# Layer 0 of a two-layer graph network: in the steps whose two MLP buffers have equal widths, one clamp and one logarithm instruction cover both

## The reference, cut to what matters

```python
def _L0_gnn_ref(x, edge_idx, W0, b0, W1, b1, W2, b2):
    row, col = (edge_idx[0], edge_idx[1])
    h = jnp.concatenate([x[row], x[col]], axis=-1)
    h = jax.nn.softplus(h @ W0 + b0)
    h = jax.nn.softplus(h @ W1 + b1)
    h = h @ W2 + b2
    return jax.ops.segment_sum(h, row, num_segments=x.shape[0])

h = jnp.maximum(_layernorm(x, axis=-1), 0.0)
x = x + _L0_gnn_ref(h, edge_index, L0_gnn_W0, ...)
```

## Time and profile before

| | us |
|---|---|
| median of 3 runs | 2696.3 |
| lowest, highest run | 2668.45, 2700.9 |
| the profiled execution | 2709.65 |
| its span, first to last instruction | 2708.0 |
| steady part of `edges0` (46 blocks) within that span | 379.3 to 1831.1 |

### The profile page before, as it was taken

The page is one execution under the profiler, slowest core; times in us unless marked ns, Lnnn a source line. Parts: engine busy times, 40 slices in busy tenths (PEclk is TensorE's granted clock), DMA queues, the critical chain, the costliest instruction groups (busy, mean ns, idle before and its releaser), DMA issues. The chain is left out here.

```text
span 2708.0 us, 37399 instructions
## 1 busy us (share of the span) xinstructions
PE 1645.4 (61%) x9524; PEld 1173.3 (43%) x9524; DVE 1475.0 (54%) x4143; ACT 977.4 (36%) x2307; POOL 1200.3 (44%) x1151
## 2 busy tenths in 40 slices
PE   0111277777777777777777777775354555645556
PEld 0111155555555655555555655554232323323334
DVE  6999556655555556555566555655233433333334
ACT  0566444444444444444444444442011111111134
POOL 0899633434333333433334433332655655655610
PEclk9999988888888878888898878887677777777775
DMA  1334213222222223222232222232222222222229
GB/s 38 111 121 125 78 43 75 60 56 58 57 56 56 64 67 61 59 58 57 64 72 58 59 56 56 56 69 56 41 51 44 50 48 44 50 45 47 50 79 307
DMA packets 345722, 183.07 MB, mean 68 GB/s; under 512 B 283916, under 2 KB 309913, under 8 KB 345671
## 3 DMA queue, kind: packets, MB, share of 16 engines
q1 hardware_dynamic: 292388, 119.46, 17.5%
q0 software_dynamic: 32928, 37.40, 8.5%
q10 hardware_dynamic: 20354, 25.65, 2.6%
HBM read 126.61 MB, written 55.79 MB: 67 GB/s over the span
## 5 line engine op out<-in xcount | busy, mean ns | idle before, releaser
L770 POOL DMA_INDIRECT fast_gathered<-h_table,fast_gather_i x588 | 569.5, 969 | 954.8 <-DVE fast_gather_i L784 787.2
L1120 POOL DMA_INDIRECT fast_gathered<-h_neighbours_table,fast_index_i x441 | 422.3, 958 | 344.8 <-issue 221.2
L791 DVE TENSOR_SCALAR fast_e<-fast_e 128x384 f32<-128x384 f32 (+1 forms) x490 | 194.9, 400 | 658.0 <-ACT fast_e L1028 582.3
L1028 ACT ACTIVATE fast_e<-bank,b_s 128x384 f32<-128x384 f32 (+1 forms) x490 | 295.2, 621 | 566.2 <-remote 306.3
L799 DVE SCALAR_TENSOR_TENSOR fast_h<-bank,b_s,fast_e 128x384 f32<-128x384 f32 (+1 forms) x490 | 303.5, 659 | 0.6 <-ACT fast_e L1035 0.6
L959 PE MATMUL bank<-fast_h,w_s 128*128 128x384 f32 (+1 forms) x490 | 275.0, 649 | 1.9 <-DVE fast_h L799 1.9
L1203 PE MATMUL bank<-fast_z_in,gw_s 128*128 128x512 f32 x98 | 92.4, 1043 | 289.3 <-ACT fast_z_in L1218 217.8
L1035 ACT ACTIVATE fast_e<-fast_e 128x384 f32<-128x384 f32 (+1 forms) x490 | 265.0, 560 | 6.9 <-issue 0.7
L945 PE MATMUL bank<-fast_in_t,w_s 128*128 128x384 f32 x294 | 163.8, 645 | 166.5 <-issue 86.4
L1218 ACT ACTIVATE fast_z_in<-node_sums 128x512 f32<-128x512 f32 x49 | 29.3, 597 | 635.2 <-DMA h_table<-prep_normed 589.8
L997 PE MATMUL node_sums<-fast_message,fast_hot 128*128 128x80 f32 x1568 | 227.5, 298 | 12.1 <-issue 12.1
(11 more groups left out here) (226 smaller groups left out, 3086.9 us busy)
## 6 DMA issues: line engine op xcount, KB each, us to landing
fast_local<-local_rows SPq DMA_DIRECT2D x49, 384.0 KB
h_neighbours_table<-fast_h_rows SPq DMA_DIRECT2D x49, 320.0 KB
fast_self_rows<-h_neighbours_table SPq DMA_DIRECT2D x49, 320.0 KB
h_table<-prep_normed ACTq DMA_DIRECT2D x49, 256.0 KB
fast_own_rows<-h_table SPq DMA_DIRECT2D x49, 256.0 KB
x_plus_h<-fast_x SPq DMA_DIRECT2D x49, 256.0 KB
finish_resid<-x_plus_h SPq DMA_DIRECT2D x49, 256.0 KB
prep_xin<-in_x SPq DMA_DIRECT2D x48, 256.0 KB
```

The lines of the kernel that those rows point to most:

```text
L770: pool.indirect_dma_start(gathered[slot][:, at:at + D], None, h0_t, bass.IndirectOffsetOnAxis(ap=gather_i[q][:, n:n + 1], axis=0))\
L791: V.tensor_scalar(e[at][:, 0:w], e[at][:, 0:w], EXP_CLAMP, None, ALU.min).then_inc(done, 1)
L1028: A(e[at][:, 0:w], psum[:, 0:w], ACT.Exp, bias=b_s[:, :]).then_inc(done, 1)
L1120: pool.indirect_dma_start(gathered[q][:, c * MW:(c + 1) * MW], None, h1_t, bass.IndirectOffsetOnAxis(ap=index_i[q][:, c:c + 1], axis=0))\
```

## The change

The two buffers of the exponentials become one buffer `e` of two halves of 512 columns (in each of two slots). In step i the first layer's exponential goes to the first half of the slot, the second layer's to the second half of the same slot. Where the two widths are equal (steps 1, 3 and 4: `is_joined`), one clamp and one logarithm instruction run over both halves. In steps 0 and 2 there are two of each as before. In a joined step both softplus instructions wait for the one logarithm (`l2_ready`), and the clamp waits for both exponentials.

```diff
-                in_t, e1, h1, e2, h2 = (t(n, [128, 512], 2) for n in ("in_t", "e1", "h1", "e2", "h2"))
+                in_t, h1, h2 = (t(n, [128, 512], 2) for n in ("in_t", "h1", "h2"))
+                e = t("e", [128, 2 * 512], 2)
...
+                def first_e(i, q):
+                    return e[slot_of(i, q)][:, 0:width(i)]
+
+                def second_e(p, q):
+                    return e[1 - slot_of(p, q)][:, 512:512 + width(p)]
+
+                def both_e(i, q):
+                    return e[slot_of(i, q)][:, :].rearrange("p (h w) -> p h w", h=2)[:, :, 0:width(i)]
+
+                def is_joined(i):
+                    return i > 0 and width(i) == width(i - 1)
...
+                        def clamp_both(i):
+                            def body(b, q, turn):
+                                dve.wait_ge(e1_ready, NU * b + i + 1)
+                                dve.wait_ge(e2_ready, NU * b + i)
+                                V.tensor_scalar(both_e(i, q), both_e(i, q), EXP_CLAMP, None, ALU.min).then_inc(m2_ready, 1)
+                            return body
+
+                        def softplus_first(i):
+                            def body(b, q, turn):
+                                if is_joined(i):
+                                    dve.wait_ge(l2_ready, NU * b + i)
+                                else:
+                                    dve.wait_ge(l1_ready, alone(b, i))
...
-                            stages += [(own_lag, clamp(i, e1, e1_ready, m1_ready)),
-                                       (p_lag, clamp(p, e2, e2_ready, m2_ready))]
+                            if is_joined(i):
+                                stages.append((own_lag, clamp_both(i)))
+                            else:
+                                stages += [(own_lag, clamp_first(i)), (p_lag, clamp_second(p))]
...
+                        def ln_both(i):
+                            def body(b, q, turn):
+                                act.wait_ge(m2_ready, NU * b + i)
+                                A(both_e(i, q), both_e(i, q), ACT.Ln, bias=1.0).then_inc(l2_ready, 1)
+                            return body
...
-                            out += [(0, ln(i, m1_ready, e1, l1_ready)), (1, ln(p, m2_ready, e2, l2_ready))]
+                            if is_joined(i):
+                                out.append((0, ln_both(i)))
+                            else:
+                                out += [(0, ln_first(i)), (1, ln_second(p))]
```

More of the change, by code:

```diff
@@ L693, in slot_of, with alone @@
                     return (NU * q + i) % 2
+                def first_e(i, q):
[6 more added lines that the diff above has]
+                    return i > 0 and width(i) == width(i - 1)
+                def alone(b, i):
+                    kinds = [n for n in range(NU) if not is_joined(n)]
+                    return len(kinds) * b + kinds.index(i) + 1
                 def width(i):
@@ L792, in clamp, with softplus_second @@
                             return body
-                        def softplus(i, psum, b_s, ln, ln_done, to, read, done):
+                        def softplus_second(p):
                             def body(b, q, turn):
[L796 to L800, removed]
+                                dve.wait_ge(l2_ready, NU * b + p + 1)
+                                wait_from(dve, raw_done, NU * b + p - 1)
+                                w, at = width(p), slot_of(p, q)
+                                V.scalar_tensor_tensor(h2[at][:, 0:w], ps_2[:, 0:w], b1_s[:, :], second_e(p, q),
+                                                       ALU.add, ALU.max).then_inc(h2_ready, 1)
@@ L1021, in take_in, with exp_first @@
                             return body
-                        def exp(i, psum, b_s, pre, read, e, done):
+                        def exp_first(i):
                             def body(b, q, turn):
[L1025 to L1028, removed]
+                                act.wait_ge(pre1_done, NU * b + i + 1)
+                                wait_from(act, h1_ready, NU * b + i - 1)
+                                A(first_e(i, q), ps_1[:, 0:width(i)], ACT.Exp, bias=b0_s[:, :]).then_inc(e1_ready, 1)
@@ L1029, in exp, with exp_second @@
                             return body
[L1031 removed]
+                        def exp_second(p):
                             def body(b, q, turn):
[L1033 to L1035 removed]
+                                act.wait_ge(pre2_done, NU * b + p + 1)
+                                wait_from(act, h2_ready, NU * b + p - 1)
+                                A(second_e(p, q), ps_2[:, 0:width(p)], ACT.Exp, bias=b1_s[:, :]).then_inc(e2_ready, 1)
+                            return body
@@ new lines, in ln_first, with body, ln_second @@
+                        def ln_first(i):
+                            def body(b, q, turn):
+                                act.wait_ge(m1_ready, alone(b, i))
+                                A(first_e(i, q), first_e(i, q), ACT.Ln, bias=1.0).then_inc(l1_ready, 1)
+                            return body
+                        def ln_second(p):
+                            def body(b, q, turn):
+                                act.wait_ge(m2_ready, NU * b + p + 1)
+                                A(second_e(p, q), second_e(p, q), ACT.Ln, bias=1.0).then_inc(l2_ready, 1)
+                            return body
```

21 lines of the change are left out of this document (14 added, 7 removed).

## The result

The changed kernel takes 2772.85 us (median of 4 runs, 2767.47 to 2790.02) against 2695.03 us (4 runs, 2668.45 to 2700.9): 1.032 times the kernel before, interval 1.024 to 1.040. It is slower by 78 us where 47 were forecast; 2773 lies inside the range of 2700 to 2785.

A forecast was written before the change was run, and what follows sets the result against it. The prediction took a ring of `indices`, gathers and steps 2, 3 and 4 as the bound. Its terms, 49 × (0.90 + 0.04) + 1 = 47 us, on a median of 2696.3 gave 2743 us, range 2700 to 2785.

The forecast's parts named there:

- slow clamp: Rival: the joined clamp takes 0.95 us, not 0.56, in steps 3 and 4; 38 us more, 2781 us; chance 0.08.
- Ring through the gathers: A block's period runs through `indices`, gathers on POOL, steps 2, 3, 4; steps 0 and 1 have some 7 us spare.
- Step 4: End of the block: softplus waits for joined clamp and logarithm, so the gathers start later; 0.90 us a block.
- Step 3: Layer 1 behind it starts 0.07 us later, the rest hidden by PE's transposes; taken as 0.04 us a block.
- Step 1: Beside the gathers: softplus 0.5 us later but hidden; nothing in 46 blocks, at most 1 us together in first and last.
- Durations: Joined instructions at two widths of 384: logarithm over 768 columns 0.84 us, clamp 0.56 us.
- The fixed cost of an instruction: Rival, joined steps: dropped fixed parts, 0.20 us a logarithm and 0.16 a clamp, save 53 us; 2643 us; chance 0.04.
- the stretch from index copy to step 2: Gathers and what follows: step 2 starts 17.1 us after the first gather, before and after the change.
- worse clock: Rival: extra waits shift blocks against PE's clock; half a microsecond a block more makes 2768 us; chance 0.06.

The follow-up runs named there:

- e12: Changed kernel with 9 gathers a block in place of 12 (output differs): 2519.53 us (one run), where the kernel before took 2703.
- e10: Kernel before with the four `dst_hots` instructions moved from step 0 to the end of step 2 of the block before: 2702.79 us against 2702.62.
- e1: Changed kernel with only step 1 joined: 2240.54 us against 2176.43 for the kernel before, ratio 1.032.
- e2: Changed kernel with only step 4 joined: 2316.8 us, ratio 1.065 to the kernel before.
- e6: The changed kernel unaltered, run again on another chip: 2328.87 us against 2176.45 for the kernel before, ratio 1.069.
- e7: Changed kernel with two clamps kept and only the logarithm joined: 2271.55 us against 2176.45 for the kernel before, ratio 1.045.
- e11: Changed kernel with the index copy moved from the end of step 4 to the end of step 3: 2930.78 us (one run).
- e5: The kernel before, unchanged, traced on another chip: 2177.13 us, ratio 1.001.

## Why the prediction came out as it did

The direction and the main term were right; the size was short by 31 us. That 2773 still lies in the range is partly luck: its upper end of 2785 was set for a slow clamp, which didn't happen. I had also given 0.57 to a change within 2% and only 0.40 to "slower", which it was.

- **Ring through the gathers.** Right on the chip of the comparison: index copy to step 2 is 18.31 us in the median (18.27 before), and e12 and e10 show both sides of it. It isn't a property of the kernel, though: on free chips it doesn't exist, and even here four blocks before came early. I had taken one trace for the machine.
- **Step 4, 0.90 us a block.** Measured 0.99 in the median. The clamp starts 0.12 us after the exponential (906.34 to 906.46) where I had 0.03 and a hundredth for the double wait. Mean 0.96, so 47 us over 49 blocks where I had 44.
- **Step 3, 0.07 us at full clock.** Measured 0.13 to 0.14, for the same 0.08. In the mean over all blocks it vanishes (5.11 to 5.07), because the clock differed: at full clock the step takes 4.50 us for 4.36 and otherwise 5.85 for 5.76, but 27 of 46 blocks ran it at full clock where 22 had.
- **Step 1, nothing.** Right where PE is held. On a free chip it costs 0.62 us of latency and, by e1, 0.9 us more, at a mean clock of 0.94 for 0.99.
- **Durations, and the slow-clamp rival.** 0.843 and 0.560 us against 0.84 and 0.56. The rule of the Trainium skill, "VectorE: DVE Perf Modes", section "What auto-detection actually checks", that the double pace survives when the outermost dimension is even: the trace agrees, 560 ns for two pieces of 384.
- **The fixed cost of an instruction.** Saved on both engines, worth nothing. The rule of the Trainium skill, "VectorE: DVE Perf Modes", section "The TRN2 errata", that each instruction pays a fixed latency, is borne out for the fixed part; it did not bound anything. I had ACT's busy time down by 27 us, and it fell by 6. The durations of ACT's instructions do add up to 26 us less (715.9 to 689.9), but neighbours overlap in the records (in the earlier trace rows the first logarithm of step 4 starts at 529.48, 0.10 before the second exponential ends), and this overlap shrank from 75 to 55 us. A good part of what was saved had run beside another instruction.
- **The term that was mis-sized: the stretch from index copy to step 2.** The sum took it as the same in every block, before and after. Between the two profiled executions the ring's mean rose by 1.28 us a block: 0.96 in step 4, 0.28 in this stretch (18.08 to 18.36), and nothing net in steps 2 and 3. Of the 0.28 (13 us in all) 10 us are the four early blocks before; after, no block came earlier than 17.6 us. Why, I didn't find.
- **The clock.** I had kept it out of the sum and given "worse clock" 0.06 at 25 us. Between these two executions it cost nothing net in steps 2 and 3. That a wait in step 4 costs clock in the steps behind is shown by e2 for a free chip; for the holding chip it isn't shown.
- **What stays open.** The remaining 20 us between 58 and 78 lie between executions of one kernel (2668 to 2710 before, 2767 to 2790 after) and have no trace to be read from.

## What to carry to other kernels

Joining two instructions saves a fixed part on engines that may be idle, and makes the first consumer wait for the second producer; count the exposed chain, not the busy time. On a chain that PE closes, price the gap also in clock: in e2, on a free chip, 1 us of wait in step 4 took 2 more. And before a wait in a trace is used as cover, look whether the same program shows it on another chip.

## What was not expected of the hardware

- One program took 2176 us on each of two chips, 2703 on a third and 2695 in the first comparison, 24% more. The mean granted clock of the whole run was 0.93 against 0.82, and on the slow ones PE was held beside the indirect gathers, in most blocks until 2.6 to 3.3 us after the last was issued (step 1: 12.1 us against 4.4). What holds PE stays open; ACT's waits name only "remote".
- A DVE instruction that waits for two semaphores started 0.11 us after the later one's producer had ended (the joined clamp in e6, median), where one that waits for a single one started 0.03 after (the second clamp in e7).
- Behind a hold, PE worked through 9.1 us without a recorded pause at a mean clock of 0.56 (e11).
- The granted clock differed by 0.10 (0.99 and 0.89) between e5 and e2 although PE's longest pause was 2.16 us in both.
